# Writing out the sixteen passes of the token layers of a conv and attention hybrid

## The chip, the cores and the metric

The kernel runs on one core of a Trainium2 chip. The metric is the device time of one execution in microseconds (us). A core has five engines, each with a sequencer that reads its own list of instructions: PE (TensorE, matmuls), DVE (VectorE), ACT (ScalarE), POOL (GpSimd) and SP (SyncE, which here issues all DMAs). Engines meet only at semaphores: an instruction raises one when it is done, another waits until it has reached a value.

## The reference, cut to what matters

The input is 16 images of 128 channels by 28x28 positions (T = 784), all fp32. Four layers are computed. Layers 0 and 1 are convolutions; the change doesn't touch them. Layers 2 and 3 take each image as T tokens of 128 channels:

```python
t = t + _L2_attn_ref(_ln_t(t), W, v)   # scores[i,j] = v . tanh(Wi[i] + Wi[j]); softmax; times tokens
t = t + _L2_ffn_ref(_ln_t(t), ...)     # 8 experts, the best 2 of each token, weighted
t = t + _L3_attn_ref(_ln_t(t), W, b)   # causal linear attention
t = t + _L3_ffn_ref(_ln_t(t), ...)     # 32 filters along the tokens, mixed by 128x128 matrices
```

The scores dominate: for every pair of tokens (by symmetry a little over half of them) a sum, a tanh and a weighted sum over 128 channels. The images are independent of each other in these layers.

## The kernel before, in words

`conv_layers` does layers 0 and 1 for all images and leaves the result in a DRAM scratch; it has a loop of its own, from another helper, which stays. `token_layers` then does layers 2 and 3 in NI = 16 passes, one for each image. Pass b works on three images at once: the scores of image b; the softmax of the later score rows, the experts and the linear attention of image b - 1; and the filters and their mixing for image b - 2.

The body of a pass is a list of NS = 135 slots, the same on all engines. In a slot DVE makes the sums (line 1420, four TENSOR_SCALARs for the wide slots, or one TENSOR_TENSOR at line 1424 for the last seven) into one of RINGS = 5 ring buffers, ACT takes their tanh in place (line 1101), and PE reduces over the channels into the bank `psS` (line 1007). Everything else of the three images is hung between slots: each helper is a generator that yields the slot after which its next piece is due, and `in_step` issues the pieces that are due. That order is written out by hand in the tables AT_...; it is a function of the slot alone. A pass ends with the corner: DVE makes a small tile of sums (line 1428), ACT its tanh (line 1104), PE 16 small matmul rows (line 1013). The next pass starts on PE only when DVE has copied the last two score blocks of the pass before out of `psS` (`last_evacs`, lines 1184 to 1189), and DVE does this after the sums of the first four slots of the new pass, since the ring lets it run four slots ahead.

How a pass is repeated is in `passes`, called once by each of the five engines with its own `one_pass`. Passes 0, 1 and 2 are written out with b a Python number. Passes 3 to 14 are a loop on the engine, `e.Fori(0, 6)`, whose body holds two passes, an odd one and an even one, since buffers alternate by the parity p; b is then `2 * bb + 3` or `2 * bb + 4`, an expression of a loop register. Pass 15 is written out again, and `last` drains. The first, second and last passes differ in content (`no(b, 0)`, `no(b, 1)`, `no(b, 2)`, `no(b, NI - 1)`); passes 3 to 14 don't. Pass 2 lacks one DVE operation of pass 3, the second half of `spectral_out`. Pass 15 lacks the preparation of a next image.

Waits go through `W` (line 647): it waits for `ev.k * b + k`. With a number this is a constant; with the loop register it is arithmetic of the sequencer (ALU_OP, FUSED_REGOPS, MOVE) ahead of the wait. Also `use` (bank turns of `psF`), the slot waits on `s_credit` (line 1415) and `Chain.sync` (line 1117, which counts DVE's own operations, K = 374 of them in two passes) depend on b or bb in this way, and so do the addresses of `load_x` and `store` (lines 702 and 715). At the end of a loop trip each engine has a compare-and-branch of its own; there is no barrier between the engines.

Of the kernel before, what the change touches and what calls it, by code (L numbers as in the profile page):

```python
# [559 lines left out]
def token_layers(nc, ai, x1, out_dram, NI):  # L560
# [10 lines left out]
    with ExitStack() as ctx:  # L571
# [96 lines left out]
        def passes(e, prologue, one_pass, last):  # L668

            prologue()  # L670
            for b in range(3): one_pass(b, b % 2)
            trips = (NI - 4) // 2
            with e.Fori(0, trips) as bb:
                one_pass(2 * bb + 3, 1, bb)
                one_pass(2 * bb + 4, 0, bb)
            one_pass(NI - 1, 1)
            last()
        no = lambda b, value: isinstance(b, int) and b == value

# [11 lines left out]
        def _(sp):  # L691
# [47 lines left out]
            def last():  # L739
                load_mix(NI - 2)  # L740
                load_mix(NI - 1)
                store(NI - 1)
            passes(sp, prologue, one_pass, last)
            W(sp, stored, 0, NI)

        @block.gpsimd
        def _(pool):
# [37 lines left out]
            def last():  # L785
                for k in range(3): root(lnv, lns, k + 1, NI - 1)
            passes(pool, lambda: root(lnv0, lns0, 1, 0), one_pass, last)

        @block.tensor
        def _(pe):  # L790
# [225 lines left out]
            def last():  # L1016
                run([soft_old(blk, NI, NI - 1, nrm2[:, 1]) for blk in range(2, 7)] + [after(NI - 1), turn_u(NI - 1), spectral(NI - 2, 0)], alone)
                run([spectral(NI - 1, 1)], alone)
            passes(pe, lambda: run([next_image(-1, 0, 0)], alone), one_pass, last)

        @block.scalar
# [460 lines left out]
```

How the kernel before makes its waits and increments, by code:

```python
        def wait(e, sem, v):  # L123
            if not isinstance(v, int) or v > 0: e.wait_ge(sem, v)
# [18 lines left out]
        @block.sync  # L143
# [8 lines left out]
            def store(p):  # L152
                sp.wait_ge(s_o, 4 * p + 4)
                sp.dma_start(x1[bass.ds(p, 1)].rearrange("a i c t -> c (a i) t"), x1o[:, :, :]).then_inc(s_st, 16)
            def one_pair(p, buf, first, last, pp=None):
                if not last:
                    wait(sp, s_x1, 4 * p)
                    wait(sp, s_x, 16 * p + 16)
                    sp.dma_start(xin2[:, 1 - buf], ai["x"][bass.ds(p + 1, 1)].rearrange("a i c t -> c (a i) t")).then_inc(s_x, 16)
                if not first: store(p - 1)
            pairs(sp, one_pair)
            store(NP - 1)
            sp.wait_ge(s_st, 16 * NP)
# [1 line left out]
        @block.gpsimd  # L167
# [3 lines left out]
            pool.memset(xn2[:, 0], 0.0).then_inc(s_pool, 1)  # L171
            pool.memset(xn2[:, 1], 0.0).then_inc(s_pool, 1)
            pool.memset(minus_half[:, :], -0.5).then_inc(s_pool, 1)
            pool.memset(x1p[:, :, :, :], 0.0).then_inc(s_pool, 1)
            pool.memset(xq[:, :, :, :], 0.0).then_inc(s_pool, 1)
            pool.wait_ge(s_pool, 7)
            pool.affine_select(out=onehot[:, :], in_=onehot[:, :], compare_op=ALU.not_equal, fill=1.0, base=-31, pattern=[[1, 63]], channel_multiplier=0).then_inc(s_pool, 1)
# [8 lines left out]
        @block.tensor  # L187
        def _(pe):
            pe.wait_ge(s_pool, 10)
            def normalize(q):
                yield AT_GN["mean"]
```

## Time and profile before

| | |
|---|---|
| median of 3 runs (lowest, highest) | 12501.48 us (12500.0, 12501.75) |
| the profiled execution | 12500.22 us |
| its span, first to last instruction | 12498.5 us |
| PE busy | 11704.8 us (94%) |
| DVE busy | 11385.2 us (91%) |
| ACT busy | 10886.1 us (87%) |
| POOL busy | 126.2 us (1%) |
| mean granted TensorE clock | 0.98 |

The profile gives for each engine how long it computed. Register, branch and semaphore instructions are not counted as busy, so sequencer work shows only as idle time put down to "issue", or, in the chain of waits, as DVEq or PEq (q for the queue of the engine). A stretch of the token layers can be asked for by its start and end in us from the span's start. I set the border of a pass at the start of DVE's corner operation (line 1428), of which there are 16, one in each pass: pass b lasts from the corner of pass b - 1 to its own. The corners lie at 6531.6, 6880.8, 7255.0, 7631.9, 8006.6, 8386.2, 8760.7, 9140.6, 9515.2, 9895.1, 10269.7, 10649.3, 11023.9, 11403.8, 11778.3 and 12147.0 us.

### The profile page before, as it was taken

The numbers are of one execution on the slowest core, as the hardware profiler recorded it, in microseconds if no ns is written. First come the engines' busy times: TensorE is split into PE (matmuls) and PEld (weight loads), VectorE is DVE, ScalarE is ACT, GpSimd is POOL, SyncE is SP. The second block draws the span as 40 slices with busy tenths as digits, with TensorE's granted clock in tenths as the row PEclk, the third lists the DMA queues.
The fourth block names the chain that finished last, engine by engine and source line by source line (L and its number), as shares of the span: only waits on it lengthen the run. The fifth ranks groups of instructions, "written<-read, shape, count | busy, mean of one in ns | idle before, by whom it ended". The sixth has DMA issues, their size and how long they took to land. (4 is left out here: it accounts for less than half of the span.)

```text
span 12498.5 us, 297675 instructions
## 1 busy us (share of the span) xinstructions
PE 11704.8 (94%) x123040; PEld 5806.2 (46%) x123040; DVE 11385.2 (91%) x21539; ACT 10886.1 (87%) x7444; POOL 126.2 (1%) x103
## 2 busy tenths in 40 slices
PE   8999999999999999999867999999999999999999
PEld 3333333333333333333323555555555555555567
DVE  9999999999999999999899888898888898989881
ACT  8999999999999999999788888888888888888872
POOL 0000000000000000000000000000000000000000
PEclk9999999999999999999978999999999999999999
DMA  0000000000000000000010111111111111111113
GB/s 14 2 7 2 4 4 2 7 2 4 4 2 7 2 4 4 2 4 2 23 45 1 50 52 51 53 53 50 50 52 52 52 54 49 50 52 53 50 57 108
DMA packets 290040, 355.08 MB, mean 28 GB/s; under 512 B 28040, under 2 KB 242960, under 8 KB 288656
## 3 DMA queue, kind: packets, MB, share of 16 engines
q1 hardware_dynamic: 288656, 335.48, 9.1%
q8 instruction: 1008, 16.52, 0.5%
q14 instruction: 376, 3.08, 0.1%
HBM read 314.14 MB, written 21.23 MB: 27 GB/s over the span
## 5 line engine op out<-in xcount | busy, mean ns | idle before, releaser
L276 ACT ACTIVATE c_ring<-c_xn,c_w_neg 128x1568 f32<-128x1568 f32 x3824 | 5791.1, 1604 | 282.3 <-PE c_acc L235 275.5
L235 PE MATMUL c_acc<-c_ring,c_onehot 128*32 128x392 f32 x68608 | 5764.9, 493 | 138.3 <-DVE c_ring L434 79.3
L1101 ACT ACTIVATE t_ring<-t_ring 128x3120 f32<-128x3120 f32 (+56 forms) x2160 | 4498.7, 2111 | 913.9 <-DVE t_ring L1420 859.1
L426 DVE TENSOR_SCALAR c_ring<-c_xn,c_w 128x1568 f32<-128x1568 f32 x4752 | 4582.2, 1051 | 95.0 <-PE c_acc L235 95.0
L1420 DVE TENSOR_SCALAR t_ring<-t_proj 128x784 f32<-128x784 f32 (+63 forms) x10240 | 3907.2, 461 | 311.0 <-PE t_psS L1007 280.0
L235 PEld LDWEIGHTS c_acc<-c_ring,c_onehot 128*32 128x32 f32 x68608 | 2217.9, 110 | 3659.2 <-issue 3211.2
L1007 PE MATMUL t_psS<-t_ring,t_vhot 128*32 128x272 f32 (+22 forms) x36864 | 2375.6, 407 | 418.3 <-ACT t_ring L1101 242.4
L1007 PEld LDWEIGHTS t_psS<-t_ring,t_vhot 128*32 128x32 f32 x36864 | 1022.5, 113 | 1650.3 <-issue 992.7
L964 PE MATMUL t_psC<-t_filter_work 128*128 128x392 f32 (+3 forms) x6144 | 1663.9, 407 | 0.0
L964 PEld LDWEIGHTS t_psC<-t_filter_work 128*128 128x128 f32 x6144 | 1105.2, 191 | 689.2 <-issue 176.2
L434 DVE SCALAR_TENSOR_TENSOR c_ring<-c_xn,c_w,c_ring 128x784 f32<-128x784 f32 x1280 | 1275.6, 1047 | 95.8 <-ACT c_ring L276 94.6
L975 PE MATMUL t_psZ<-t_filter_work 128*128 128x98 f32 (+2 forms) x4096 | 842.8, 349 | 42.6 <-ACT t_filter_work L1088 42.6
L1088 ACT ACTIVATE t_filter_work<-t_psC 128x392 f32<-128x392 f32 x1024 | 494.8, 483 | 252.3 <-PE t_psC L964 252.3
L975 PEld LDWEIGHTS t_psZ<-t_filter_work 128*128 128x128 f32 x4096 | 619.1, 195 | 189.8 <-issue 57.4
L1336 DVE SCALAR_TENSOR_TENSOR t_tok_after<-t_psB,t_side,t_tok_after 128x128 f32<-128x128 f32 (+1 forms) x896 | 312.1, 348 | 84.8 <-PE t_psB L889 60.6
L889 PE MATMUL t_psB<-t_ew,t_nrmT 128*128 128x512 f32 x448 | 233.5, 605 | 0.0
L835 PE MATMUL t_psF<-t_nrm,t_ET 128*128 128x129 f32 (+3 forms) x1568 | 222.5, 287 | 3.7 <-ACT t_ET L1049 3.7
L1424 DVE TENSOR_TENSOR t_ring<-t_proj 128x2880 f32<-128x2880 f32 (+6 forms) x112 | 203.6, 1865 | 9.8 <-PE t_psS L1007 9.5
L835 PEld LDWEIGHTS t_psF<-t_nrm,t_ET 128*128 128x128 f32 (+3 forms) x1568 | 185.6, 178 | 26.0 <-ACT t_ET L1049 6.6
L772 POOL TENSOR_TENSOR t_rstd<-t_var,t_half 128x7 f32<-128x7 f32 x64 | 108.1, 1689 | 6059.9 <-DVE t_var L1268 6059.9
L1389 DVE TENSOR_TENSOR t_filter_work<-t_filter_work,t_psZ 128x392 f32<-128x392 f32 x32 | 19.4, 607 | 150.0 <-PE t_psZ L975 150.0
L201 PE MATMUL c_pst<-c_x1p,c_wq 128*128 128x392 f32 x448 | 155.3, 499 | 0.7 <-DVE c_x1p L373 0.7
(231 smaller groups left out, 3340.1 us busy)
## 6 DMA issues: line engine op xcount, KB each, us to landing
t_filter_work<-in_toep_dram SPq DMA_DIRECT2D x256, 393.0 KB, 3.3
t_filter_work<-mix_scratch SPq DMA_DIRECT2D x512, 192.0 KB, 2.5
t_filter_work<-in_toep_dram SPq DMA_DIRECT2D x256, 197.0 KB, 2.8
t_filter_work<-mix_scratch SPq DMA_DIRECT2D x512, 64.0 KB, 1.8
mix_scratch<-t_filter_work SPq DMA_DIRECT2D x4, 2048.0 KB, 9.5
c_xin<-in_x_dram SPq DMA_DIRECT2D x8, 784.0 KB, 4.4
x_scratch<-c_x1o SPq DMA_DIRECT2D x8, 784.0 KB, 3.4
t_proj<-x_scratch SPq DMA_DIRECT2D x16, 392.0 KB, 3.2
```

The source lines that it names most:

```text
L235: mm = pe.matmul(acc[32 * g:32 * g + 32, ch, 0:HALF], onehot[:, 31 - r:63 - r], ring[:, s % RING, g, ch * HALF:(ch + 1) * HALF], start=(s ...
L276: ins = act.activation(tile4(ring[:, s % RING, g, :]), window(xn, tap), ACT.Relu, bias=w0_neg[:, tap, 4 * r + g:4 * r + g + 1])
L426: dve.tensor_scalar(tile4(ring[:, s % RING, g, :]), window(xn, tap), w0[:, tap, 4 * r + g:4 * r + g + 1], 0.0, ALU.subtract, ALU.max).then ...
L434: dve.scalar_tensor_tensor(out=half, in0=xn[:, im, TAP_B // 3:TAP_B // 3 + HW, TAP_B % 3:TAP_B % 3 + HW], scalar=w0[:, TAP_B, 4 * r + g:4 ...
L835: ins = pe.matmul(psF[0:R, 0:129], ET[0:TOK_ROWS[t], t, 0:R], nrm[0:TOK_ROWS[t], t, :], start=(t == 0), stop=(t == 6))
L964: ins = pe.matmul(out[:, :, c0 - t0:t1 - t0], U[:, src, i, :], toep[:, j % FILTS, :, 1 - shift + c0 - 128 * i:1 - shift + t1 - 128 * i], s ...
L975: ins = pe.matmul(sums2(lo, hi, t0), mixr[:, m % MIXES, s, :], UT[:, 2 * j % UTS:2 * j % UTS + 2, QUART * f + lo - t0:QUART * f + hi - t0] ...
L1007: ins = pe.matmul(psS[32 * q:32 * q + 32, at + lo:at + hi], vhot[:, 31 - r:63 - r], ring[:, st % RINGS, c + lo:c + hi], start=(r == 0), st ...
L1088: act.activation(UT[:, u % UTS, :], psC[:, u % 2, 0:HALF], ACT.Copy).then_inc(eC.s, 1)
L1101: act.activation(ring[:, st % RINGS, 0:n], ring[:, st % RINGS, 0:n], ACT.Tanh).then_inc(th.s, 1)
L1336: ins = dve.scalar_tensor_tensor(out=tokA[0:R, t, :], in0=psB[0:R, 512 * h + 128 * e:512 * h + 128 * e + 128], scalar=prob[0:R, t, 4 * h + ...
L1420: dve.tensor_scalar(ring[:, st % RINGS, o + q * w:o + (q + 1) * w], proj[:, 128 * blk + first:T], proj[:, i:i + 1], None, ALU.add).then_in ...
```

## The change

In `passes`, the three written-out passes, the loop and the last written-out pass become one Python loop over all NI passes. Each engine's list then holds sixteen passes in a row, b is a number in each, so every wait has a constant and every address is fixed, and no engine branches in the token layers. The order of the instructions that compute is the same, and so are tiles, buffers and the tables of slots. `Chain` no longer counts by turns, since `c.turn` stays None.

```diff
         def passes(e, prologue, one_pass, last):
 
             prologue()
-            for b in range(3): one_pass(b, b % 2)
-            trips = (NI - 4) // 2
-            with e.Fori(0, trips) as bb:
-                one_pass(2 * bb + 3, 1, bb)
-                one_pass(2 * bb + 4, 0, bb)
-            one_pass(NI - 1, 1)
+            for b in range(NI): one_pass(b, b % 2)
             last()
         no = lambda b, value: isinstance(b, int) and b == value
```

## Rows read from the trace of the kernel before

**Rows 1.** The page: span, busy time and count by engine, DMA queue of the instructions.
```profile
span 12498.5 us, 297675 instructions
PE 11704.8 (94%) x123040; PEld 5806.2 (46%) x123040; DVE 11385.2 (91%) x21539; ACT 10886.1 (87%) x7444; POOL 126.2 (1%) x103
...
q8 instruction: 1008, 16.52, 0.5%
```

**Rows 2.** Windows, one a pass: stretch, length, busy PE, PEld, DVE, ACT, POOL, clock, DMA.
```profile
6880.78:7255.04 374.26, 350.23 (x3351) 214.18 (x3347) 336.80 (x930) 314.14 (x221) 7.13 (x4) 0.98 0.18 51
7255.04:7631.91 376.87, 352.59 (x3365) 216.27 (x3359) 337.49 (x931) 315.91 (x224) 6.74 (x4) 0.98 0.18 52
7631.91:8006.56 374.65, 351.67 (x3366) 215.94 (x3359) 337.50 (x931) 315.64 (x224) 6.74 (x4) 0.98 0.18 52
8006.56:8386.16 379.60, 351.66 (x3366) 215.99 (x3359) 337.47 (x931) 316.10 (x224) 6.74 (x4) 0.98 0.18 51
...
9515.15:9895.13 379.98, 354.01 (x3368) 217.45 (x3361) 337.44 (x932) 317.26 (x226) 6.73 (x4) 0.97 0.18 51
...
11403.83:11778.33 374.50, 351.53 (x3363) 215.94 (x3359) 337.38 (x931) 314.40 (x222) 6.73 (x4) 0.98 0.19 55
```

**Rows 3.** Waits of DVE, passes 3 to 14: us in total, times, longest.
```profile
DVE t_ring L1420 <- PE t_psS L1007: 229.0, 217, 2.6
...
DVE t_ring L1420 <- issue: 12.9, 5, 2.7
```

**Rows 4.** Chain of waits at the first taken branch: start, us, what.
```profile
8006.37 0.06 DVEq L673
...
8006.56 0.42 DVE t_corner L1428
8006.98 2.37 issue
8009.35 0.09 DVEq L673
```

**Rows 5.** Timeline of DVE behind the same branch, start and us first.
```profile
8009.60 8.64 DVE L1420 TENSOR_SCALAR t_ring<-t_proj 128x784 f32<-128x784 f32 x16 [2.62 <-issue]
```

**Rows 6.** Timeline of DVE from pass 3 to 4, inside the loop's body.
```profile
7631.91 0.42 DVE L1428 TENSOR_TENSOR t_corner<-t_proj 128x256 f32<-128x256 f32 x1
7632.46 8.65 DVE L1420 TENSOR_SCALAR t_ring<-t_proj 128x784 f32<-128x784 f32 x16
```

**Rows 7.** Timeline of DVE from pass 2 to 3, at the loop's entry.
```profile
7255.05 0.42 DVE L1428 TENSOR_TENSOR t_corner<-t_proj 128x256 f32<-128x256 f32 x1
7255.60 8.65 DVE L1420 TENSOR_SCALAR t_ring<-t_proj 128x784 f32<-128x784 f32 x16
```

**Rows 8.** Timeline of PE behind the taken branch.
```profile
8018.76 2.84 PE L1007 MATMUL t_psS<-t_ring,t_vhot 128*32 128x512 f32 x16 [6.21 <-DVE t_S L1184]
```

**Rows 9.** Timeline of PE from pass 3 to 4, its first matmuls.
```profile
7641.59 2.39 PE L1007 MATMUL t_psS<-t_ring,t_vhot 128*32 128x512 f32 x12 [3.69 <-DVE t_S L1184]
```

**Rows 10.** Windows over the first matmuls of passes 4 and 5.
```profile
7639.00:7659.00 20.00, 16.35 (x141) 7.66 (x145) 18.83 (x39) 20.00 (x9) 0.00 (x0) 0.91 0.18 61
8016.00:8036.00 20.00, 16.26 (x129) 7.47 (x133) 18.00 (x39) 19.81 (x9) 0.00 (x0) 0.83 0.20 67
```

**Rows 11.** Windows over the same 12 us of passes 3 and 4.
```profile
7552.90:7564.90 12.00, 9.89 (x85) 5.15 (x85) 9.83 (x28) 8.04 (x6) 0.00 (x0) 0.86 0.18 52
7929.80:7941.80 12.00, 9.96 (x93) 5.75 (x94) 11.38 (x32) 8.60 (x7) 0.00 (x0) 1.00 0.17 52
```

**Rows 12.** Timeline of DVE in that stretch, pass 3 and pass 4.
```profile
7559.11 0.29 DVE L1364 TENSOR_TENSOR t_side<-t_psB,t_causal 128x128 f32<-128x128 f32 x1 [1.03 <-PE t_psB L913]
...
7934.26 0.28 DVE L1364 TENSOR_TENSOR t_side<-t_psB,t_causal 128x128 f32<-128x128 f32 x1
```

## The prediction, made before the changed kernel ran

> **What bounds the kernel now.** I read the page first, then the token layers cut into passes, then the seam between two passes in the chain of waits and in the timelines of DVE and PE, because the change touches nothing but seams and waits. In the page the reader is to see that PE, DVE and ACT are all nearly full [rows 1]: this is a pipeline of three engines, and time is saved only where all three stand. The windows, one for each pass, say how much there is to save [rows 2]. Passes 3 to 14 do the same work, yet they come in two kinds. The even ones (4, 6 up to 14, six of them) take 374.50 to 374.65 us. The odd ones behind a taken branch (5, 7, 9, 11, 13) take 379.60 to 379.98 us. Pass 3, the first odd one, with no branch ahead of it, takes 376.87 us. Busy DVE is 337.4 to 337.5 us in all of them, so the difference is waiting. The 12 passes together last 11778.33 - 7255.04 = 4523.3 us.
>
> The waits of DVE in these passes show the rule and the exception: it mostly waits for PE to free a ring buffer (229.0 us, 217 times), and exactly 5 times, 12.9 us in all, for nothing that the profile shows ("issue") [rows 3]. Five is the number of taken branches of a loop of six trips. The chain at the first of them has it on the path that sets the end: DVE's branch takes 0.06 us, the corner operation that was queued behind it runs, and then come 2.37 us of nothing before DVE's queue is heard of again [rows 4].
>
> **The change part by part.**
>
> *DVE's restart.* Behind the taken branch, from the corner's start at 8006.56 to the first sum at 8009.60, 3.04 us go by [rows 4, 5]. Inside the body, from pass 3 to 4, the same two operations are 7632.46 - 7631.91 = 0.55 us apart [rows 6], and at the loop's entry, where the lists run straight on too, 7255.60 - 7255.05 = 0.55 us [rows 7]. So a taken branch costs DVE 2.5 us here. The idle time before the sums was 2.62 us there against 12.9 / 5 = 2.58 on average [rows 3, 5], so I take 5 x 2.45 = 12.2 us for the five. All of this is on the path: the sums feed ACT and PE, and the ring was empty. Nothing takes its place: in rows 6 and 7 the next sum follows at once.
>
> At this place a rule of the Trainium skill bears. The trace shows 0.06 us for DVE's branch itself and 2.37 us of silence behind it [rows 4]. "Advanced Engine Details and Errata", section Control Flow Timing, gives some 108 ns for a compare-and-branch; by that alone the five trips would be worth about 0.5 us and the change nothing. "Runtime: NRT & Kernel Launch", section Instruction fetch mechanics, says that a taken branch whose target is not in the small instruction memory must first fetch it by DMA. The silence in the trace agrees with the second; the first covers only the 0.06.
>
> *PE's restart.* PE stands 6.21 us ahead of its first matmul of pass 5, put down to DVE's copy out of `psS` [rows 8], against 3.69 us at the seam without a branch [rows 9]. The difference, 2.5 us, is DVE's own lateness, since PE waits for DVE there (the last copies come after the sums of four slots). Whatever PE's branch costs lies under this wait, and is gone with it: 0 us more, and if that cover were missing the most that it could be is the 6.2. ACT, SP and POOL branch as well; ACT's next input is DVE's sums, and SP and POOL run ahead. I take 0 for them.
>
> *What the seam costs beyond the restart.* An odd pass behind a branch is 379.8 - 374.6 = 5.2 us longer than an even one [rows 2]. DVE's restart explains 2.45. The other 2.7 us are PE at the lower of its two clocks. Over the first matmuls the granted clock is 0.83 in pass 5 and 0.91 in pass 4 [rows 10]; and near the end of pass 3, which has no branch, 12 us have a clock of 0.86 where the same 12 us of pass 4 have 1.00 [rows 11], and DVE waits 1.03 us for the matmuls of line 913 that it did not wait for in pass 4 [rows 12]. PE was short of work just before both places. So the dips have two parts. One follows the longer idle time behind a branch and must go. The other falls or doesn't by where the pass lies in time: pass 3 pays 2.25 us of it without any branch. In the kernel before, the odd passes lay alike and the even ones alike, because two passes took the same 754 us each time. When the odd ones become shorter by several us this breaks, and each pass draws anew.
>
> Bounds: all 12 passes like the even ones gives 12 x 374.6 = 4495.2, a gain of 28.1 us. The six odd ones like pass 3 gives 6 x 374.6 + 6 x 376.9 = 4509.0, a gain of 14.3 us. All 12 like pass 3 gives 4522.4, a gain of 0.9 us. Pass 3 itself lies where it lay before and pays its 2.3 again. For the others I have rows at two places in time only, one that pays nothing (the even passes) and one that pays 2.3 (pass 3). I let half of the 12 passes pay, and since most of these will lie between the two places I give them 1.7 us each, nearer to pass 3: 4495.2 + 6 x 1.7 = 4505.4. Gain of the loop's stretch: 4523.3 - 4505.4 = 17.9 us, of which 12.2 is the restart and 5.7 the clock.
>
> *Constants for registers in the waits.* The trace has one pair for this: pass 2 is written out and pass 4 is in the loop. Pass 2 took 374.26 us, with one DVE operation fewer (336.80 busy against 337.50, so 0.7 us), pass 4 took 374.65 [rows 2]. So the same pass with constants would have taken 374.3 to 375.0: between 0.4 us less and 0.3 us more than in the loop, for 12 passes -4 to +4 us. It is 0 by the nearer reading: the arithmetic is done by the sequencers ahead of full queues, behind instructions of 0.6 us. If that cover is gone it shows only behind an empty queue, as at the seam, and there both kinds take the same 0.55 us [rows 6, 7]. I take 0. Fixed addresses of the loads and stores: SP is not on the path; 0.
>
> *Longer lists.* PE's list streams in before and after: the queue of the instructions moved 16.52 MB for 246,080 executed matmuls and weight loads, 67 bytes for each [rows 1], so the loop's body came anew in each trip and was not kept. A straight list asks for no more. I take 0; rival C has the other side.
>
> **Sum.** Against the profiled execution (12500.22 us, span 12498.5): 12500.2 - 12.2 - 5.7 = 12482.3. The median of the runs was 12501.48, 1.3 more than the profiled one; I add this: 12483.5 us, a gain of 18 us or 0.14%. A measurement of this kernel can tell about 0.2% (25 us) from no change, so this counts as the same.
>
> **The rivals.**
>
> *A. The clock dips go altogether (27 in 100).* If all of the odd passes' excess hangs on the branch, also that of pass 3 through where the loop begins, the 12 passes come to 374.6 each: gain 28, time 12473 us, just faster by over 0.2%. For it: even passes never pay. Against it: pass 3 pays 2.25 us with no branch ahead. It decides from a mean of 375.0 a pass on.
>
> *B. The change doesn't do what it says in time: only the restart is won (15 in 100).* All places in time cost like pass 3, so that the clock takes back what the shorter seam gives: 12 x 376.87 = 4522.4, time 12500.5. For it: of 12 passes only those at one place in time were cheap. Against it: passes 2 and 4 are at the cheap place, and the odd ones can't all be worse off than with longer idle time. The middle of this, gain 8 to 12, is the likelier part of it: 12491.
>
> *C. The straight list is fetched late (4 in 100).* The price of one late fetch on the path is the 2.45 us of DVE. If in each pass two fetches fell on an emptied queue, 12 x 2 x 2.45 = 59 us would come and 18 go: 12543 us. It turns the sign from 18 / 2.45 = 8 such stalls on. Against it: the "issue" waits of DVE in this stretch number 5, all behind branches [rows 3], though a body of two passes is as long as the straight list over two passes, and pass 2, written out, has no such loss [rows 2]. "Runtime: NRT & Kernel Launch", section Instruction fetch mechanics, calls the sequential fetch hidden; passes 2 and 4 agree, being within 0.4 us.
>
> **How the numbers follow.** The forecast has 54 in 100, A 27, B 15, C 4. Range: A's lower end with the constants' 4 us is 12469; B's middle is 12491 and its upper part reaches 12500, of which I leave out the far part and C: 12469 to 12494. Faster by over 0.2% means under 12476.5: A and the edge of the forecast, 0.29. Slower by over 0.2% means over 12526.5: C's upper part, 0.03. The same: 0.68.
>
> **What would show it.** Right: no "issue" wait of DVE between 7255 us and the end of pass 14; corner to first sum 0.55 us at every seam; PE's idle time at a seam about 3.7 us everywhere; lengths of 374.5 to 377 us in an order that is no longer odd and even; total of passes 3 to 14 near 4505. Wrong in the clock term: all passes at 374.6 (A) or at 376.9 (B). Wrong in the constants: passes with no clock dip that differ from 374.6 by more than 0.4 us. Wrong altogether: new "issue" waits inside a pass (C), or the 0.55 us at a seam having grown.

## The result and the profile after

The written-out kernel takes 12484.99 us, median of 22 runs (12480.27 to 12486.52); the kernel before takes 12501.52 (12495.76 to 12509.44, 22 runs). The ratio is 0.9986, 95% interval 0.9980 to 0.9993: 16.5 us less, 0.13%, small but clear of no change. The forecast was 12483.5. Its profiled execution took 12485.33 us with a span of 12483.6, 14.9 under the span before.

First the windows, one for each pass, with the same columns and borders (DVE's corner operation) as [rows 2]: passes 2 to 5, 14 and 15.

```profile
6881.60:7258.07 376.47, 352.28 (x3361) 215.64 (x3357) 336.90 (x930) 315.79 (x223) 10.18 (x4) 0.97 0.18 50
7258.07:7632.24 374.17, 351.58 (x3364) 215.77 (x3360) 337.19 (x931) 314.34 (x222) 6.63 (x4) 0.98 0.18 52
7632.24:8008.27 376.03, 351.01 (x3365) 215.64 (x3360) 337.39 (x932) 315.80 (x224) 6.62 (x4) 0.99 0.18 52
8008.27:8384.38 376.11, 353.08 (x3367) 216.89 (x3362) 337.46 (x932) 317.21 (x226) 10.18 (x4) 0.98 0.18 52
...
11385.52:11760.99 375.47, 351.09 (x3367) 214.72 (x3360) 337.31 (x932) 315.79 (x224) 6.63 (x4) 0.98 0.19 55
11760.99:12132.19 371.20, 350.03 (x3347) 214.28 (x3342) 332.55 (x905) 315.48 (x221) 4.97 (x3) 0.97 0.18 51
```

The reader is to see three things. The rhythm of odd and even is gone, and with it every pass near 380. Passes 3 to 14 together take 11760.99 - 7258.07 = 4502.9 us, 20.4 less than before. And passes that hold the very same list in both kernels moved: pass 2 took 374.26 before and 376.47 now, pass 15 368.64 and now 371.20. Up to the end of pass 2 the new profile is 3.0 us behind and pass 15 adds 2.6, so 14.9 of the 20.4 are left in the span. Of the 3.0, 1.7 already lie ahead of the first corner, where neither list was changed; in the profiles of this document that corner starts anywhere from 6530.7 to 6533.3 us.

Where the clock is at its lower level can be set against these lengths. The total of it does not order the passes: pass 4 took 376.03 us with 10.2 us at the lower level, pass 3 took 374.17 with 13.6. The place goes with it. Lined up operation by operation, DVE loses 1.7 us in pass 4 against pass 3 between 301 and 304 us behind the border, which is nearly the whole difference, and none elsewhere that lasts. These are the same 8 us of the two passes, 299 to 307 us behind the border:

```profile
7557.07:7565.07 8.00, 7.32 (x78) 3.57 (x79) 7.30 (x23) 5.65 (x4) 0.00 (x0) 1.00 0.21 66
7931.24:7939.24 8.00, 7.25 (x53) 3.54 (x57) 5.70 (x14) 4.28 (x4) 0.00 (x0) 0.79 0.16 52
```

In pass 5 a loss of 1.8 us lies at 372 to 374 us, in 6.8 us of lower clock from 368.5 on (3.4 us in pass 3), and in pass 12 one of 1.3 us has come up by 19.4 us, behind 6.8 us of lower clock from 8.5 on (again 3.4 in pass 3). The granted clock belongs to PE, and in each of these places DVE waits for PE's results.

The timelines of DVE and PE at the seam from pass 4 to 5, where [rows 4, 5] and [rows 8] had a taken branch:

```profile
8008.27 0.42 DVE L1423 TENSOR_TENSOR t_corner<-t_proj 128x256 f32<-128x256 f32 x1
8008.89 8.65 DVE L1415 TENSOR_SCALAR t_ring<-t_proj 128x784 f32<-128x784 f32 x16 [0.20 <-PE t_psS L1002]
...
8017.94 2.51 PE L1002 MATMUL t_psS<-t_ring,t_vhot 128*32 128x512 f32 x16 [3.74 <-DVE t_S L1179]
```

Corner to first sum is 0.62 us (3.04 before), and PE stands 3.74 us (6.21 before). The five "issue" waits of DVE of [rows 3] have no counterpart left in the same stretch. The two queues that carry instructions moved a little less than before (1008 packets in [rows 1] on the first; the second went from 376 packets to 293):

```profile
q8 instruction: 988, 16.19, 0.5%
```

### The profile page after: what moved, and what is told of

It reads as the page before. It is cut to its first block and busy times, and to the rows that moved or that the text cites. A ratio compares the mean times of both kernels' runs of the same rounds, so it can differ in the third digit from the quotient of the medians.

```text
span 12483.6 us, 288268 instructions
## 1 busy us (share of the span) xinstructions
PE 11697.6 (94%) x123040; PEld 5796.6 (46%) x123040; DVE 11383.7 (91%) x21539; ACT 10886.6 (87%) x7444; POOL 135.4 (1%) x103
```

## The experiments

Each was timed in five rounds beside the kernel before, which took 12499.8 to 12502.0 in these sets. One set can differ from another by 1 to 2 us, so what counts are differences of 4 us and more, and what the profiles show of single passes. The 95% interval of a ratio is wide, some 11 us to either side; the ranges of the runs part the kernels better: 12480.3 to 12486.5 us written out, 12493.8 and more for the kernel before. Of each change to the program the main lines are shown.

**Registers without a branch, first try.**

```diff
-            for b in range(NI): one_pass(b, b % 2)
+            for b in range(3): one_pass(b, b % 2)
+            trips = (NI - 4) // 12
+            with e.Fori(0, trips) as bb:
+                for i in range(12): one_pass(12 * bb + 3 + i, (1 + i) % 2, bb)
+            one_pass(NI - 1, 1)
```

> Passes 3 to 14 are the body of a loop of one trip: no branch is taken, but waits and addresses come from the loop's register as in the kernel before. It parts the two halves of the change. Theory: the arithmetic costs 0.3 to 0.4 us a pass (in the two profiles the cheapest passes are 374.50 to 374.65 us in the loop and 374.17 to 374.31 written out), so the cheapest passes read 374.5 to 374.65 again, DVE has no wait put down to issue at a seam, and the time is some 4.5 us above the changed kernel: 12489. Rival: the arithmetic is free and the 0.4 us is chance; cheapest passes 374.2, time 12485. Second rival: the seam itself was dearer with registers; corner to first sum over 0.6 us.

12482.69 us (ratio 0.9986, 0.9977 to 0.9996). `Chain`'s count of operations was set to the longer body as well. It can't part the two theories: the trace holds 7,223 register instructions (ALU_OP and FUSED_REGOPS, the arithmetic on registers), against 7,218 written out and 17,838 in the kernel before, so the waits of a loop of one trip had been turned into constants; only a compare-and-branch that is not taken is left on each engine. It is a second copy of the written-out kernel, and as such it shows something else. The window of its pass 11:

```profile
10256.17:10631.66 375.49, 351.01 (x3365) 214.58 (x3360) 337.27 (x931) 315.78 (x224) 6.62 (x4) 0.98 0.18 52
```

Ten passes in a row, 5 to 14, took 375.36 to 375.49 us, with the granted clock at its lower level at the same two places in each, for 6.8 us from 8.4 to 8.7 and from 271.2 to 271.5 us behind the border. A pass of the same list can also take 374.14 us (pass 3 here), and the same lists gave other lengths in passes 4 to 10 of the first profile (374.19 to 376.11). The passes had fallen into step with the clock's dips (these stretches at the lower level), at a length that is not their shortest.

**One engine in the loop.** In all three, the named engines keep the loop of before and the rest is written out.

```diff
+            if not (e is nc.vector):            # second: nc.tensor; third: ACT, SP and POOL
+                for b in range(NI): one_pass(b, b % 2)
+                last()
+                return
             for b in range(3): one_pass(b, b % 2)
```

> Only DVE keeps the loop of six trips; the other four engines have all passes written out. Theory: DVE's restart is the whole cost of the taken branches, so corner to first sum is 2.8 to 3.2 us at five seams, 12 us come back in all, and with DVE's share of the register arithmetic the time is 12497 to 12501. Rival: PE's refetch (its branch took over 6 us in the profile of before, under a wait for DVE) was part of the price through the clock or the queue; then this kernel keeps only some 6 to 9 us of loss: 12491 to 12494.

12502.92 us (ratio 1.0003, 0.9994 to 1.0012; runs 12496.9 to 12506.9). The whole gain is gone, and a little more than was expected. Corner to first sum reads 2.82 to 3.11 us at the five seams.

> Only PE keeps the loop; the other four are written out. Behind a taken branch PE stands over 6 us from the end of its list, and without DVE's lateness its next work is due some 3.7 to 5 us after the corner's matmuls. Theory as predicted (0 us because it lay under DVE's wait): false as soon as DVE is on time: PE is then late by 6.5 - 4 = 2 to 2.5 us at five seams, a loss of 10 to 12 us, of which the ring gives little back: 12493 to 12497. Rival: the stall stays hidden, time 12485 to 12487.

12499.57 us (ratio 1.0000, 0.9991 to 1.0009; runs 12494.4 to 12502.8). Nearly the whole gain is gone here too, more than the 12 us that the theory allowed. PE's timeline at the seam from pass 4 to 5 of this kernel, then its waits between 7255 and 11760 us (in total, times, longest):

```profile
8013.07 1.16 PE L1017 MATMUL t_psS<-t_corner,t_vhot 128*32 128x16 f32 x32
8020.68 3.69 PE L1011 MATMUL t_psS<-t_ring,t_vhot 128*32 128x512 f32 x20 [6.45 <-ACT t_ring L1105]
```

```profile
PE t_psS L1011 <- issue: 23.0, 5, 7.2
```

and DVE's, in the same kernel:

```profile
8017.72 0.15 DVE L1188 COPY t_S<-t_psS 16x16 f32<-16x16 f32 x1
8017.80 2.18 DVE L1424 TENSOR_SCALAR t_ring<-t_proj 128x768 f32<-128x768 f32 x4
8023.59 0.62 DVE L1424 TENSOR_SCALAR t_ring<-t_proj 128x764 f32<-128x764 f32 x1 [3.60 <-PE t_psS L1011]
```

DVE is on time here, its copies out of `psS` are done at 8017.87, and PE starts only at 8020.68, 2.8 us later. DVE fills what is left of the ring and then stands 3.60 us. The label of PE's wait (ACT) names an engine that had long been done: PE's own COMPARE_BRANCH stands in the trace from 8013.6 us for 6.78 us, up to 0.3 us before these matmuls. At the other four seams the wait is 5.08, 5.33, 4.63 and 7.20 us and stands in the group "issue". PE starts 11.1 to 13.2 us behind the border at the five seams, 12.0 on average, for 9.75 at nearly all others. So PE's restart reaches past DVE's copies by 2.2 us on average, about as much as DVE's own restart costs. The two lay side by side, and each alone costs what both cost together. This kernel's median less that of the written-out one, 14.6 us, is more than 5 x 2.2 = 11; where the rest arises is not settled.

> ACT, SP and POOL keep the loop; DVE and PE, each of which alone brought back nearly the whole loss (12502.9 and 12499.6 us), are written out. Theory: these three branch under cover (ACT's next input is DVE's fifth sum, SP and POOL run ahead), so the time is that of the written-out kernel, 12482 to 12487. Rival: ACT's fetch of 2.5 us holds the tanh of the corner or of the first ring and so PE: 12488 to 12495.

12487.53 us (ratio 0.9987, 0.9978 to 0.9996), 2.5 us above the written-out kernel and at the edge of what was expected. Corner to first sum stays 0.62 us. ACT's restart just fits under PE's wait for DVE: behind its branch it stands 2.8 to 3.2 us ahead of its first ring tile, where it went on at once when written out, and at one seam PE waits for it, 3.89 us for 3.74. Whether the 2.5 us are ACT's is not settled. In the trace of the kernel before, POOL's branch is different from all others: its body holds 18 recorded instructions, and the next follows 0.12 us behind a taken branch. SP, with 340, needs 2.7 to 2.9 us, ACT, with 1,011, 2.5 to 2.9.

**A taken branch to a near target.**

```diff
             for b in range(NI):
                 one_pass(b, b % 2)
+                if b in (4, 6, 8, 10, 12):
+                    with e.Fori(0, 2) as turn: e.nop(nofuse=True)
```

> The written-out kernel with an empty loop of two trips on each engine at the five seams where the loop of before branched: the same number of taken branches, but each to a target a few instructions back. Theory: the price is the fetch of a distant target, not the branch; corner to first sum grows by under 0.5 us at these seams and the time by under 2.5 us: 12485 to 12488. Rival: any taken branch throws away what was fetched ahead; then 2 to 2.5 us at five seams return and the time is 12496 to 12500.

12482.78 us (ratio 0.9987, 0.9977 to 0.9996). The trace has ten executed branches more on each engine, five of them taken (the nop left no record). On DVE one takes 50 to 63 ns and the next instruction of the list follows 0.14 us behind a taken one. Corner to first sum stays at 0.62 us. A branch costs nothing here; going back over a long body does, and POOL's short body says the same. Refetch is this document's name for that silence; no run separates the fetch itself.

**One taken branch, registers kept.**

```diff
-            trips = (NI - 4) // 2
+            trips = (NI - 4) // 6
             with e.Fori(0, trips) as bb:
-                one_pass(2 * bb + 3, 1, bb)
-                one_pass(2 * bb + 4, 0, bb)
+                for i in range(6): one_pass(6 * bb + 3 + i, (1 + i) % 2, bb)
```

> The loop has six passes in its body and two trips, on all engines: one taken branch (ahead of pass 9) instead of five, and waits from registers in all 12 passes, which the loop of one trip turned out not to have. Two things are disputed now. First the price of a branch: 3.5 to 5 us at pass 9, once. Second the registers: if the arithmetic costs 0.4 us a pass and times add, the passes without a branch sum to 4 to 5 us more than written out, and the time is 12490 to 12493. Theory now held: the passes fall into step with the dips of the clock (in the one-trip kernel eight in a row took 375.43 to 375.49 us with dips at the same two places), so 0.4 us a pass is swallowed: passes 5 to 8 and 11 to 14 again at 375.4 to 375.5, time 12485 to 12488.

12490.95 us (ratio 0.9992, 0.9983 to 1.0001). DVE's waits in the loop's stretch:

```profile
DVE t_ring L1419 <- issue: 2.7, 1, 2.7
...
DVE t_small L1208 <- DVE t_S L1227: 2.6, 12, 0.2
```

The runs lie at 12486.8 to 12494.3, above all of the written-out kernel's and below all of the kernel before's in this set. The refetch is there once, in pass 9, which took 379.20 us. The other eleven average (4513.8 - 379.2) / 11 = 375.9 us, against 4502.9 / 12 = 375.2 written out. So the additive theory had the time right; that the step of the clock would swallow the cost was wrong here. Not all of the 0.7 us a pass need be the registers', since lengths were drawn anew here as well. The second line shows a place where it arises. DVE copies a piece of the scores and takes a row maximum from it, with waits on its own work between. The same pair of operations in pass 12 before and in pass 6 written out:

```profile
10668.93 0.68 DVE L1228 COPY t_S<-t_psB 128x512 f32<-128x512 f32 x1
10669.82 0.97 DVE L1209 TENSOR_REDUCE t_small<-t_S 128x1 f32<-128x784 f32 x1 [0.21 <-DVE t_S L1228]
```

```profile
8403.96 0.68 DVE L1223 COPY t_S<-t_psB 128x512 f32<-128x512 f32 x1
8404.68 0.97 DVE L1204 TENSOR_REDUCE t_small<-t_S 128x1 f32<-128x784 f32 x1
```

0.21 us stand between them with registers and none with constants. This wait appears 12 times in all kernels whose DVE loops and in none whose DVE is written out. The cheapest passes give the best estimate of the whole amount: 374.50 to 374.65 us in the kernel before and 374.57 to 374.64 with DVE alone in the loop, against 374.17 to 374.31 written out and 374.34 with PE alone in the loop. That is 0.3 to 0.4 us a pass, nearly all of it DVE's.

**A cost put ahead of the first sum.** Three kernels add chained memsets of one column to the written-out kernel: three in each of passes 3 to 14, eight once in pass 3, eleven in each of passes 3 to 14.

```diff
                 proj = proj2[:, p]
+                if 3 <= b <= 14:                # eight: if no(b, 3)
+                    for i in range(3): c.link(dve.memset(pad[:, 5:6], 0.0))   # or 8, or 11
```

> The written-out kernel with three small DVE operations in a chain (a memset of one column, each waiting for the one before) ahead of the first sum of passes 3 to 14: about 0.4 us more on DVE's path in each pass. Additive theory: 12 x 0.4 = 5 us more than the one-trip kernel, passes at 375.9, time 12488 to 12490. Theory of step: the pass stays at 375.4 to 375.5 once it has fallen into it, the dips at the same offsets, only the seam grows; time 12482 to 12485.

12482.81 us (ratio 0.9986, 0.9977 to 0.9995). The three operations moved the first sum by only 0.11 us (0.73 behind the border for 0.62), so this tells nothing apart. Its passes went round in threes, 376.1, 376.1 and 374.2 us, again 375.5 on average.

> The written-out kernel with eight such operations once, ahead of pass 3: 1 us of shift and nothing else. Additive theory: pass lengths as in the changed kernel, time 1 us more. Theory of place: passes 3 and 4 take other lengths than 374.2 and 376.0 (between 374 and 377), and within some five passes the length settles at 375.4 to 375.5 as if nothing had been; time 12481 to 12487.

12485.16 us (ratio 0.9987, 0.9978 to 0.9996). The first sum of pass 3 came 0.73 us later. Pass 3 took 376.17 us, then pass 4 was at 375.43 and passes 5 to 14 at 375.43 to 375.49. In the profile of the loop of one trip, where the first low stretch of pass 3 also starts 9.3 us behind the border, passes 3 and 4 took 374.14 and 374.31. A shift of under a microsecond, once, changes the lengths of the passes behind it, and they settle again. Lengths belong to a place in time, not to a place in the list.

> The written-out kernel with eleven chained small DVE operations ahead of the first sum of passes 3 to 14. Three cost only 0.11 us a pass (corner to first sum 0.73 for 0.62), which told nothing apart; eleven should put the first sum at 1.7 us, 1.1 us later. Additive theory: 12 x 1.1 = 13 us more than the written-out kernels (12483 to 12485), so 12496 to 12498. Theory of step: the passes go on at a mean of 375.4 to 375.6 us, now with fewer losses to low clock in each, and the time is 12482 to 12488.

12489.66 us, median (ratio 0.9992, 0.9983 to 1.0001), and neither theory fits all of it. The runs fall in two groups, 12479.9 to 12489.7 (six) and 12503.1 to 12504.1 (five). The profiled one was of the upper group; windows of passes 11 and 12 of it:

```profile
10273.12:10649.74 376.62, 351.00 (x3366) 214.59 (x3360) 337.90 (x942) 316.03 (x224) 6.62 (x4) 0.98 0.18 51
10649.74:11027.49 377.75, 351.42 (x3365) 215.60 (x3360) 338.02 (x943) 316.02 (x224) 6.63 (x4) 0.98 0.18 51
```

Ten passes, 5 to 14, lie in pairs of 754.2 to 754.4 us. The pairs of the kernel before, an odd and an even one, were 379.60 + 374.58 = 754.2 up to 379.98 + 374.52 = 754.5: nearly the same, with other costs inside. The lower group is where the kernel without any added cost is. So one and the same cost of 1.1 us a pass (PE stands 4.86 us at the seam for 3.74) is worth nothing in one run and 20 us in the next. The low stretches repeat with the pairs, at about 9.8 and 272.6 us behind the border in the shorter pass, at 8.6, 302.2 and 370.4 in the longer. That the clock's dips hold a pass to a few lengths fits all of this; no run shows their part alone, since none could hold the clock still.

**Copies one slot earlier, a version that beats both.** PE's 3.7 us at every seam are a wait for DVE's last copies, and PE has scored the corner 5.9 us behind the border.

```diff
             def last_evacs(d):
-                yield -1
+                yield -2                        # next kernel but one: -3
                 evac(5, d); evac(6, d)
```

> The written-out kernel with DVE's last copies of a pass (blocks 5 and 6) due one slot earlier, after three slots of sums instead of four. PE stands 3.74 us at every seam for these copies, so it starts 2.1 us earlier in each of 15 passes. If PE's start is what a pass waits for (PE's corner ends 5.9 us after the border, so the copies can be made from then on), 1 to 2 us a pass are won: 12460 to 12472, the pass at about 373.5. Theory of step: the dips may hold the pass at 375.4 to 375.5 all the same (no gain), or let it fall to a length in which they lie elsewhere, 372 to 372.5 us. Rival: DVE gives back later what PE wins, since the ring is what DVE waits for; under 0.5 us a pass, 12478 to 12485.

12464.90 us, seven runs from 12462.1 to 12468.7 (ratio 0.9972, 0.9961 to 0.9983): 20 us under the written-out kernel and 36 under the one before. PE at its seam from pass 4 to 5:

```profile
8006.61 3.09 PE L1002 MATMUL t_psS<-t_ring,t_vhot 128*32 128x512 f32 x32 [1.61 <-DVE t_S L1179]
```

It stands 1.61 us for 3.74. Passes 3 to 14 take 373.43 to 375.18 us, 4491.9 together.

> The kernel before, loop and all, with the last copies of a pass one slot earlier, which took the written-out kernel from 12485 to 12464.9. If the two edits are independent it saves 20 us here too: 12481. If PE's own refetch (over 6 us from the end of its list) is what a seam behind a branch waits for once DVE is earlier, the five branched seams gain nothing and the others 1 to 1.5 us each: 12486 to 12491.

12497.12 us (ratio 0.9996, 0.9987 to 1.0005). The same edit in the loop kernel saves only some 5 us, less than the least expected. Its PE behind the taken branch:

```profile
8015.84 4.54 PE L1007 MATMUL t_psS<-t_ring,t_vhot 128*32 128x512 f32 x24 [6.13 <-issue]
```

The wait has become "issue": at these five seams the refetch decides. At the other seams PE does start 2.1 us earlier, yet the six even passes took 3.5 us more than before together. Four of them, at 375.5 to 375.6 us, have a stretch of low clock about 300 us behind the border; lined up with pass 8, which has none there and took 373.90, pass 4 falls 1.7 us behind at 301 to 303 us, as in the written-out kernel. Only with the passes written out are the earlier copies worth 20 us.

> The written-out kernel with these copies two slots earlier than first. DVE reaches them 4.9 us after the border, 1 us before PE has scored the corner (5.93 us), so DVE stands 1 us at each seam; PE's idle time falls from 1.62 us to about 0.7. If PE's start counts, 0.3 to 0.9 us a pass more are won than with one slot: 12452 to 12461. If DVE's stand counts as much, 12463 to 12470.

12482.29 us (ratio 0.9984, 0.9975 to 0.9993), 17 us worse than one slot. DVE now comes too early:

```profile
8009.99 0.38 DVE L1182 TENSOR_TENSOR t_S<-t_psS,t_half 128x128 f32<-128x128 f32 x1 [0.95 <-PE t_psS L1008]
```

It stands 0.95 us for the corner's scores, with only eight sums made ahead. Passes 3 to 14 took 4503.6 us, 11.7 more than with one slot, and this wait totals 13.9 us there. Both expectations were missed: PE stands only 0.59 us at the seam, a microsecond less, and nothing of that reaches the end.

## Why the prediction was right, and which of its steps were not

That the median came within 1.5 us of the forecast is luck in part. In the profiles the loop's stretch gained 20.4 us for 17.9, 5.6 were lost outside for 0, and the two medians are 16.5 apart where the two profiles are 14.9. What was right is that DVE's restart goes and that the lengths draw anew.

**DVE's restart, 12.2 us.** Seen as forecast: the "issue" waits are gone, the seam reads 0.62 us instead of 0.55 (the 0.07 is a constant wait that stands as an instruction of its own). As a measure of worth it was read too simply, since taking DVE out of the loop while PE stays in it (the kernel where PE loops alone) leaves 12499.57.

**PE's restart, "0 us more".** This step failed. The row that put PE's 6.21 us down to DVE's copy was true for the kernel before, where both came at the same moment, but it said nothing on how far PE's own refetch reached beneath it. PE's own branch took 6.3 to 6.9 us there, and a PE that loops alone stands 4.6 to 7.2 us: it decides as soon as DVE is on time. In the sum it did no harm only because the change frees both.

**The clock, 5.7 us.** The kind was right: the lengths drew anew and averaged 4502.9 / 12 = 375.24 us, where 375.45 was forecast. The size hides two errors that cancel. The passes lie further above the cheapest than I gave them, 375.24 - 374.2 = 1.0 us each for the 0.85, and the cheapest are 0.4 us cheaper by the registers. Two readings under it failed. Pass 3 was to pay its 2.3 us again and took 374.17. And of the dip over the first matmuls I wrote that it follows the longer idle time behind a branch and must go. Pass 3 of the kernel before, with no branch ahead, has it as deep, and so has pass 12 of the written-out kernel:

```profile
7262.00:7282.00 20.00, 16.30 (x132) 7.40 (x135) 18.22 (x39) 20.00 (x9) 0.00 (x0) 0.83 0.21 70
10641.59:10661.59 20.00, 16.21 (x125) 7.38 (x129) 17.80 (x38) 20.00 (x9) 0.00 (x0) 0.83 0.18 60
```

PE stood 3.74 us there both times. What an odd pass paid beyond DVE's restart shows when pass 5 is lined up with pass 6, both before: 0.8 us are lost by 19 us behind the border, and 1.9 at 302 to 304 us. That passes stay in step at one length, the reason for both kernels' regularity, I had only as "lay alike".

**Registers, 0 us.** Wrong by 12 x 0.3 to 0.4 = 3.6 to 4.8 us of gain, about the bound of 4. The comparison of pass 2 with pass 4 failed because pass 2's own length moves by 2.2 us with its place in time: of the eleven profiles in which it is the same list, five have it at 373.99 to 374.28 us and six at 376.35 to 376.47, while the reason given, full queues, doesn't hold where DVE waits on its own last operation.

**Outside the loop, 0 us.** Wrong by 5.6 us of loss in the profile: 2.2 in pass 2, which drew the longer of its two lengths, 2.6 in pass 15, and 0.8 up to the end of pass 1. It need not come from the change: the kernel with three memsets, written out as well, drew the short pass 2, 374.04 us.

**Longer lists.** Right: no new "issue" wait of DVE; rival C had no support. Rival A would have needed every pass at 374.6, B at 376.9; the mean lay between.

By parts, from medians of different sets and so to 1 or 2 us: four taken branches less are worth 12501.5 - 12490.95 = 10.6 us, and the last one with the registers 12490.95 - 12484.99 = 6.0.

## What to carry to other kernels

A wait names only what came last: before its length is priced as the named engine's, look for what else ends at the same moment beneath it, and undo the parts one engine at a time. Going back over a long loop body cost PE, DVE, ACT and SP microseconds each, a branch to a near target nothing; and the seam is worth a second look once the refetch is gone, since a hand-set due time there may only now decide. Where pass lengths repeat to a tenth of a microsecond above their shortest value, small gains and losses need not add up.

## What the runs showed of the hardware

A pass of 135 slots settled at 375.36 to 375.49 us for up to eleven passes in a row, although the same list can run in 374.14, and a cost of about 1 us a pass left the time at 12480 to 12490 us in six runs and at 12503 to 12504 in five. A stretch of low clock 301 to 304 us behind the border went with 1.7 us lost in the pass; passes with as many such stretches elsewhere took 374.2 us. Behind a taken branch over a long body PE's matmuls stood for up to 7.2 us and DVE for up to 2.7; POOL, with a body of 18 instructions, went on 0.12 us behind it. On DVE a wait computed from a register behind its own last operation cost 0.21 us, and behind a taken branch to a near target the next instruction of the list followed in 0.14 us.
